# Self-attention with unscaled exponentials: sums by a matmul with ones, outputs divided, transposes one step sooner

## What is computed

```python
x = x + tanh(g_xattn) * xattn(layernorm(x), ctx, Wq, Wk, Wv, Wo)
x = x + tanh(g_ffn) * ffn(layernorm(x), ...)
# in ffn:
q, k = rope(q, k)
scores = einsum('bqhd,bkhd->bhqk', q, k) * 32 ** -0.5
attn = softmax(where(causal, scores, min))
ctx = einsum('bhqk,bkhd->bqhd', attn, v)      # 8 batches, 16 heads, 100 x 100
x = x + ctx @ wo
# then the router, two of eight experts for each token, and a shared expert
```

## Time and profile before

| | before |
|---|---|
| median of 3 runs | 976.92 us (974.06 to 979.06) |
| the profiled execution | 981.73 us |
| its span, first to last instruction | 979.9 us |
| mean granted clock of TensorE | 0.956 of full speed |
| PE busy | 901.8 us (92%) |
| DVE busy | 654.4 us (67%) |
| ACT busy | 565.6 us (58%) |
| POOL busy | 397.8 us (41%) |

### The profile page before, as it was taken

The page is one execution under the profiler, slowest core; times in us unless marked ns, Lnnn a source line. Parts: engine busy times, 40 slices in busy tenths (PEclk is TensorE's granted clock), DMA queues, the critical chain, the costliest instruction groups (busy, mean ns, idle before and its releaser), DMA issues.

```text
span 979.9 us, 16173 instructions
## 1 busy us (share of the span) xinstructions
PE 901.8 (92%) x5713; PEld 836.0 (85%) x5713; DVE 654.4 (67%) x1466; ACT 565.6 (58%) x1455; POOL 397.8 (41%) x373
## 2 busy tenths in 40 slices
PE   5999999999999999999879888799857989999996
PEld 4889999999989999999857766598857989999896
DVE  3557776742637777742696956666855788898863
ACT  3656666644546666653344756545335767777661
POOL 3432222345432322336654421044462555565431
PEclk9999999999999999999997989699978999999999
DMA  5766710025530000006322111022486989999875
GB/s 150 210 231 187 208 52 2 11 73 148 160 101 16 1 2 1 12 28 175 92 79 65 44 46 42 12 87 86 131 275 197 280 270 318 286 302 306 252 195 149
DMA packets 118040, 129.41 MB, mean 132 GB/s; under 512 B 13188, under 2 KB 81228, under 8 KB 117360
## 3 DMA queue, kind: packets, MB, share of 16 engines
q1 hardware_dynamic: 98862, 104.74, 34.6%
q0 software_dynamic: 5120, 10.22, 5.2%
q10 hardware_dynamic: 13978, 13.41, 4.7%
HBM read 110.81 MB, written 26.19 MB: 140 GB/s over the span
## 4 chain that ended last, share of the span: by engine, by line
PE 61%; DVE 16%; DMA 9%; issue 5%; ACT 5%; POOL 3%; ACTq 0%; POOLq 0%; DVEq 0%; SPq 0%
PE bank L2012 55%; PE bank L2141 4%; DMA s_sum<-yo,target 2%; DMA eraw<-in_L_ffn_w_down_e_dram 2%; DVE we L1339 2%; ACT we L905 1%; DVE PQ L1520 1%; POOL s_rows L1942 1%; DMA s_rows<-HR,idx 1%; DVE HR L1336 1%; DVE PQ L1518 1%; DVE sm L1543 1%; DMA eraw<-in_L_ffn_w_gate_e_dram 1%; DMA sums<-s_sum 1%; DVE wf L1339 1%
## 5 line engine op out<-in xcount | busy, mean ns | idle before, releaser
L1902 POOL TENSOR_SCALAR SC<-SC,mx,anyv 100x361 f32<-100x361 f32 x128 | 81.4, 646 | 211.2 <-DVE mx L1451 200.9
L1873 POOL TENSOR_TENSOR wf<-raw,wf 128x512 fp32r<-128x512 f32 x54 | 72.6, 1350 | 138.2 <-ACT wf L891 138.2
L1885 POOL TENSOR_TENSOR we<-eraw,we 128x704 fp32r<-128x704 f32 x40 | 74.1, 1852 | 99.5 <-ACT we L905 99.4
L1873 POOL TENSOR_TENSOR wx<-raw,wx 128x512 fp32r<-128x512 f32 x64 | 83.2, 1311 | 76.0 <-ACT wx L891 75.8
L905 ACT ACTIVATE we<-eraw 128x704 fp32r<-128x704 f32 (+2 forms) x140 | 96.8, 718 | 28.1 <-DMA eraw<-in_L_ffn_w_down_e_dram 13.1
L1339 DVE TENSOR_TENSOR we<-eraw,we 128x704 fp32r<-128x704 f32 (+2 forms) x100 | 92.8, 944 | 22.6 <-ACT we L905 22.4
L2012 PE MATMUL bank<-H2h,wf 128*128 128x400 f32 x352 | 99.7, 351 | 0.0
L1021 ACT ACTIVATE SC<-SC,mx 100x361 f32<-100x361 f32 x128 | 75.4, 593 | 29.3 <-DVE mx L1447 28.9
L2012 PE MATMUL bank<-XTh,wx 128*128 128x400 f32 x256 | 72.3, 356 | 3.7 <-POOL wx L1873 2.3
L1339 DVE TENSOR_TENSOR Kl<-bank,Kh 128x362 fp32r<-128x362 f32 x64 | 34.1, 535 | 60.3 <-ACT Kh L979 60.3
L1339 DVE TENSOR_TENSOR QOl<-bank,QOh 128x200 fp32r<-128x200 f32 (+1 forms) x96 | 41.5, 432 | 46.2 <-ACT QOh L934 36.2
(11 more groups left out here) (259 smaller groups left out, 2784.0 us busy)
## 6 DMA issues: line engine op xcount, KB each, us to landing
raw<-s_unit SPq DMA_DIRECT2D x60, 256.0 KB, 3.7
eraw<-in_L_ffn_w_gate_e_dram SPq DMA_DIRECT2D x40, 352.0 KB, 4.1
eraw<-in_L_ffn_w_up_e_dram SPq DMA_DIRECT2D x40, 352.0 KB, 5.4
eraw<-in_L_ffn_w_down_e_dram SPq DMA_DIRECT2D x40, 256.0 KB, 5.8
raw<-in_L_xattn_Wq_dram SPq DMA_DIRECT2D x32, 256.0 KB, 3.1
raw<-in_L_xattn_Wo_dram SPq DMA_DIRECT2D x32, 256.0 KB, 2.9
s_rows<-Z SPq DMA_DIRECT2D x6, 800.0 KB
XB<-s_rows ACTq DMA_DIRECT2D x18, 256.0 KB, 5.6
```

The costliest lines, as they stand in the source:

```text
L1873: eng.tensor_tensor(w[:, 1, :, :], raw[plan.raw[stream, u] % 4][:, :, :], f32(w[:, 0, :, :]), ALU.subtract).then_inc(sem("pool_w"), 1)
L1885: eng.tensor_tensor(w[0:rows, 1, 0:n], eraw[u % 6][0:rows, 0:n], f32(w[0:rows, 0, 0:n]), ALU.subtract).then_inc(sem("pool_e"), 1)
L1902: eng.tensor_scalar(sc, sc, m[:, 3, h:h + 1], anyv[:, b:b + 1], ALU.mult, ALU.mult).then_inc(sem("pool_p"), 1)
```

## The change

The exponentials are no longer scaled by the inverse of their sums before the transposes. ACT's exponentials drop the accumulated sums; DVE's reciprocal of 100x4 and its multiply of 100x400 go. Instead `f_out` is made in two parts of two columns of heads each, in steps `4q + 6` and `4q + 7`. In each part four matmuls with a tile of ones (`ones32`, 100x32) write the sums of the exponentials into one half of bank 4, spread over the 32 partitions of their head, and eight matmuls write the outputs into the other half. DVE takes the reciprocal of the 128x200 sums and multiplies the 128x200 outputs into an SBUF tile `CD` (two of them); ACT copies it to `CXh`, and DVE, one step later, subtracts for `CXl`, now from two SBUF tiles. The next part waits until the last one is divided out of bank 4.

The transposes move from step `u + 3` to `u + 2`, wait for the exponentials alone, and all use bank 3, so each waits for the copy of the one before. On ACT the exponentials now stand first in a step, then the copy of the turned rows, then `CXh`. No DMA moves. POOL fills `ones32` with one memset early on, and the counts that wait for its constants shift by one. Where the later stage takes over banks 3 and 4 it waits for `dve_ft` and `dve_cd`.

```diff
@@ steps and tables
-CONST = {"zero": 1, "eps": 3, "pad": 7, "causal": 10, "router": 11, "numbers": 19, "orders": 25, "split": 27}
+CONST = {"zero": 1, "eps": 3, "pad": 7, "causal": 10, "router": 11, "ones": 12, "numbers": 20, "orders": 26, "split": 28}
...
+    CDS = Region(nc, A2.at, A2.end)
+    CD = CDS.ring("CD", 2, [128, 2, T])
+    ones32 = CDS.place("ones32", [T, FD])
@@ -1091,28 +1094,26 @@
                            scale=scale).then_inc(sem("act_f"), 1)
 
         def self_attention(n):
-            u = n - 3
+            if n < 32:
+                act.wait_ge(sem("dve_fn"), n + 1)
+                if n >= 4:
+                    act.wait_ge(sem("pe_ft"), n - 3)
+                p, m, bank = PF[n % 4], sm[n % 4], score_bank[n % 4]
+                for c in range(4):
+                    e = eng.activation(p[:, c, :], bank[0:T, c * T:(c + 1) * T], ACT.Exp, bias=m[:, c:c + 1], scale=-1.0)
+                e.then_inc(sem("act_fe"), 1)
+            u = n - 2
             if 0 <= u < 32 and u % 2 == 0:
                 act.wait_ge(sem("pe_ft"), u + 1)
                 if u >= 6:
-                    act.wait_ge(sem("pe_fo"), (u - 6) // 4 + 1)
-                eng.activation(flat(PTf[u % 6][:, :, :]), banks[3 + u % 2][0:T, 0:4 * T], ACT.Copy).then_inc(sem("act_ft"), 1)
-            u = n - 4
-            if u >= 0 and u % 4 == 3:
-                h, b = divmod(u // 4, HB)
-                act.wait_ge(sem("pe_fo"), u // 4 + 1)
-                src = banks[4][:, 0:4 * T].rearrange("p (a b) -> p a b", a=4)
-                eng.activation(CXh[h][:, :, batch_slice(b)], src, ACT.Copy).then_inc(sem("act_cx"), 1)
-            u = n
-            if u < 32:
-                act.wait_ge(sem("dve_fn"), u + 1)
-                if u >= 4:
-                    act.wait_ge(sem("pe_ft"), u - 3)
-                p, m, bank = PF[u % 4], sm[u % 4], score_bank[u % 4]
-                for c in range(4):
-                    e = eng.activation(p[:, c, :], bank[0:T, c * T:(c + 1) * T], ACT.Exp, bias=m[:, 1, c:c + 1],
-                                       scale=-1.0, accum_out=m[:, 2, c:c + 1])
-                e.then_inc(sem("act_fe"), 1)
+                    act.wait_ge(sem("pe_fo"), 2 * ((u - 6) // 4 + 1))
+                eng.activation(flat(PTf[u % 6][:, :, :]), banks[3][0:T, 0:4 * T], ACT.Copy).then_inc(sem("act_ft"), 1)
+            if n >= 6 and n % 4 >= 2:
+                part = 2 * ((n - 6) // 4) + n % 2
+                h, b = divmod(part // 2, HB)
+                act.wait_ge(sem("dve_cd"), part + 1)
+                at = slice(part % 2 * 2, part % 2 * 2 + 2)
+                eng.activation(CXh[h][:, at, batch_slice(b)], CD[part % 2][:, :, :], ACT.Copy).then_inc(sem("act_cx"), 1)
 
         def po(h, m):
             act.wait_ge(sem("pe_po"), h * KD + m + 1)
@@ -1538,34 +1539,43 @@
             m, bank = sm[u % 4], score_bank[u % 4]
             dve.wait_ge(sem("pe_fs"), u + 1)
             if u >= 4:
-                dve.wait_ge(sem("dve_fp"), u - 3)
+                dve.wait_ge(sem("act_fe"), u - 3)
             src = bank[0:T, 0:4 * T].rearrange("p (a b) -> p a b", a=4)
-            eng.tensor_reduce(m[:, 1, :], src, AX, ALU.min).then_inc(sem("dve_fn"), 1)
+            eng.tensor_reduce(m[:, :], src, AX, ALU.min).then_inc(sem("dve_fn"), 1)
+
+        def low_of(part):
+
+            h, b = divmod(part // 2, HB)
+            at = slice(part % 2 * 2, part % 2 * 2 + 2)
+            dve.wait_ge(sem("act_cx"), part + 1)
+            low(CXl[h][:, at, batch_slice(b)], CD[part % 2][:, :, :], CXh[h][:, at, batch_slice(b)]).then_inc(sem("dve_cx"), 1)
 
         def self_attention(n):
             if n == 0:
                 f_max(0)
-            u = n - 3
+            if n >= 7 and n % 4 in (3, 0):
+                low_of(2 * ((n - 7) // 4) + (n + 1) % 2)
+            u = n - 2
             if 0 <= u < 32 and u % 2:
                 dve.wait_ge(sem("pe_ft"), u + 1)
                 if u >= 6:
-                    dve.wait_ge(sem("pe_fo"), (u - 6) // 4 + 1)
-                eng.tensor_copy(flat(PTf[u % 6][:, :, :]), banks[3 + u % 2][0:T, 0:4 * T]).then_inc(sem("dve_ft"), 1)
-            u = n - 4
-            if u >= 0 and u % 4 == 3:
-                h, b = divmod(u // 4, HB)
-                dve.wait_ge(sem("act_cx"), u // 4 + 1)
-                src = banks[4][:, 0:4 * T].rearrange("p (a b) -> p a b", a=4)
-                low(CXl[h][:, :, batch_slice(b)], src, CXh[h][:, :, batch_slice(b)]).then_inc(sem("dve_cx"), 1)
-            u = n - 1
-            if 0 <= u < 32:
-                p, m = PF[u % 4], sm[u % 4]
-                dve.wait_ge(sem("act_fe"), u + 1)
-                chained(eng.reciprocal(m[:, 3, :], m[:, 2, :]))
-                r4 = m[:, 3, :].rearrange("p (a o) -> p a o", o=1).broadcast_to([T, 4, T])
-                eng.tensor_tensor(p[:, :, :], p[:, :, :], r4, ALU.mult).then_inc(sem("dve_fp"), 1)
+                    dve.wait_ge(sem("pe_fo"), 2 * ((u - 6) // 4 + 1))
+                eng.tensor_copy(flat(PTf[u % 6][:, :, :]), banks[3][0:T, 0:4 * T]).then_inc(sem("dve_ft"), 1)
             if n + 1 < 32:
                 f_max(n + 1)
+            if n >= 6 and n % 4 >= 2:
+                part = 2 * ((n - 6) // 4) + n % 2
+                h, b = divmod(part // 2, HB)
+                dve.wait_ge(sem("pe_fo"), part + 1)
+                if part >= 2:
+                    dve.wait_ge(sem("dve_cx"), part - 1)
+                cd = CD[part % 2]
+                sums = banks[4][:, 2 * T:4 * T].rearrange("p (a b) -> p a b", a=2)
+                outs = banks[4][:, 0:2 * T].rearrange("p (a b) -> p a b", a=2)
+                chained(eng.reciprocal(cd[:, :, :], sums))
+                eng.tensor_tensor(cd[:, :, :], outs, cd[:, :, :], ALU.mult).then_inc(sem("dve_cd"), 1)
+            if n == 8 * HB + 3:
+                low_of(2 * B - 1)
 
         def er(h, i):
             b = h * HB + i
@@ -1907,6 +1917,7 @@
         def ffn_constants():
             pool.wait_ge(sem("pe_wo"), 32)
             eng.memset(WR[:, :, :], 0.0).then_inc(sem("pool_const"), 1)
+            eng.memset(ones32[:, :], 1.0).then_inc(sem("pool_const"), 1)
             for i in range(NE):
                 eng.memset(io8[:, :, i:i + 1], float(NE - i)).then_inc(sem("pool_const"), 1)
             eng.memset(ones[:, :], 1.0).then_inc(sem("pool_const"), 1)
@@ -2276,42 +2287,43 @@
                     if c == 3:
                         e.then_inc(sem("pe_fs"), 1)
 
-        def f_out(q):
+        def f_out(q, part):
 
             h, b = divmod(q, HB)
             pe.wait_ge(sem("act_ft"), 2 * q + 2)
             pe.wait_ge(sem("dve_ft"), 2 * q + 2)
             pe.wait_ge(sem("dve_v"), HB * (h + 1))
-            if q:
-                pe.wait_ge(sem("dve_cx"), q)
+            pe.wait_ge(sem("pool_const"), CONST["ones"])
+            if q or part:
+                pe.wait_ge(sem("dve_cd"), 2 * q + part)
             else:
                 pe.wait_ge(sem("dve_ht"), B - 1)
-            for c in range(4):
+            for i in range(4):
+                mm(banks[4][32 * i:32 * i + 32, 2 * T:4 * T], ones32[:, :],
+                   flat(PTf[(4 * q + i) % 6][:, 2 * part:2 * part + 2, :]), True, True)
+            for cc in range(2):
+                c = 2 * part + cc
                 for i in range(4):
                     at = (4 * c + i) * FD
-                    e = mm(banks[4][32 * i:32 * i + 32, c * T:(c + 1) * T], V[h][:, b, at:at + FD],
+                    e = mm(banks[4][32 * i:32 * i + 32, cc * T:(cc + 1) * T], V[h][:, b, at:at + FD],
                            PTf[(4 * q + i) % 6][:, c, :], True, True)
             e.then_inc(sem("pe_fo"), 1)
 
         def self_attention(n):
-            u = n - 3
+            u = n - 2
             if 0 <= u < 32:
-                pe.wait_ge(sem("dve_fp"), u + 1)
-                if u < 2:
+                pe.wait_ge(sem("act_fe"), u + 1)
+                if u == 0:
                     pe.wait_ge(sem("dve_v"), HB)
-                    pe.wait_ge(sem("dve_ht"), B - 1)
-                elif u % 2 == 0:
-                    pe.wait_ge(sem("act_ft"), u // 2)
+                elif u % 2:
+                    pe.wait_ge(sem("act_ft"), u // 2 + 1)
                 else:
                     pe.wait_ge(sem("dve_ft"), u // 2)
-                    if u >= 5:
-                        pe.wait_ge(sem("dve_cx"), (u - 5) // 4 + 1)
                 for c in range(4):
-                    e = eng.transpose(banks[3 + u % 2][0:T, c * T:(c + 1) * T], PF[u % 4][:, c, :], ident[0:T, 0:T])
+                    e = eng.transpose(banks[3][0:T, c * T:(c + 1) * T], PF[u % 4][:, c, :], ident[0:T, 0:T])
                 e.then_inc(sem("pe_ft"), 1)
-            u = n - 4
-            if u >= 0 and u % 4 == 3:
-                f_out(u // 4)
+            if n >= 6 and n % 4 >= 2:
+                f_out((n - 6) // 4, n % 2)
             if n == 0:
                 f_scores(0, 0)
             if n % 4 == 0 and n < 32:
@@ -2321,7 +2333,7 @@
 
```

(6 more changed lines are left out.)

## The result

| | before | after |
|---|---|---|
| median of 4 runs each | 977.99 us (974.06 to 979.9) | 999.95 us (997.12 to 1003.31) |
| ratio | | 1.0212, 95% interval 1.0183 to 1.0241 |
| profiled execution, span | 981.73, 979.9 us | 1000.78, 998.7 us |
| busy PE, DVE, ACT | 901.8, 654.4, 565.6 us | 910.7, 656.8, 554.4 us |
| mean granted clock | 0.956 | 0.954 |

What follows compares the result with a forecast made beforehand. DVE was taken to lead from 538 to 558 and 600 to 628 us, PE from 558 to 600. Terms 1.5 + 1.7 + 1.5 + 2.7 = +7.4 us on 976.9 gave 984.3 us, range 971 to 992 (8 in 10).

Steps and rivals of the forecast that it cites:

- four terms of the sum: Losses for 538 to 560, 560 to 600, 600 to 628 and 628 to 637 us: +1.5, +1.7, +1.5, +2.7 us.
- the middle readings: Estimates of one 128x200 reciprocal on DVE from smaller ones, 1.15 us and 1.4 us; 1.3 was taken between them.
- the cheap: Rival for all attention stages: reciprocal 0.36 us; 971.1 us if PE also keeps its clock, chance 0.14, otherwise 975.3, chance 0.15.
- dear rival: Rival for all attention stages: reciprocal at 8.5 ns an element, 0.55 us more each; 990.5 us, chance 0.20.
- Stage 538 to 560: Attention beside the second half's rotary work: division delays CXh, exponentials, copy and PE's transposes, twice; +1.5 us.
- The ring: In 538 to 560: division, CXh, weight and Q/K copies, exponentials, turned-row copy, transposes wait in a loop; PE idles 2.6 us.
- Stage 560 to 600: Stretch led by PE up to po: two further output parts, with steps 17 to 19 and po's wait even; +1.7 us.
- the first rival: All attention stages: division at 0.36 us and PE's upper clock held from 576 to 591; 971.1 us, chance 0.14.
- Stage 600 to 628: Stretch led by DVE: work +2.0 us, partly absorbed by 3 us of idle, rows' root waiting up to 1; +1.5 us.
- The end: 628 to 637 us, steps 33 to 35: second output part waits until the first is divided out of bank 4; +2.7 us.
- The second: All attention stages: reciprocal at 8.5 ns an element; +13.6, 990.5 us, up to 2 more if the clock falls; chance 0.20.
- The third: In 538 to 560 the ring doesn't close, giving up to 3 us back; sum +2.9, 979.8 us, chance 0.16.

Runs made afterwards that it cites:

- the filled version: Changed kernel with spare matmuls on PE, 56 each ahead of the transposes of steps 9 and 13 and 60 ahead of the first po group; 994.92 us, ratio 1.0157.

## Why the prediction was wrong

The direction and the places were right. All four terms of the sum were too small: the chain was priced as if PE ran at its upper clock inside it, and DVE's idle from 600 to 628 was taken to shrink where it grew.

- **Prices of the parts, right.** For the division 1.3 us was taken, 1.402 measured; the middle readings of the earlier trace rows were the right ones, and the prices of the cheap and the dear rival both fell. Measured growth from the four-element reciprocal (168 ns) is (1402 - 168) / 196 = 6.3 ns an element. An output part takes 0.82 us at the upper clock (538.24 to 539.06), 0.83 taken. The estimate of 1.67 us from the Trainium skill, VectorE: DVE Perf Modes, section "First, the fixed hardware budget", was too high. The prediction says that its rows do not reach that estimate, but the dearest of them, 8.5 ns an element, lay above it.
- **Stage 538 to 560, the step that failed: 1.5 forecast, 4.7 to 6.9 measured.** The ring was walked at the upper clock: 561.2 - 548.4 = 12.8 us a round, and with the clock held it does take 13.3. But PE's group, transposes and output part lie inside the ring, and behind an idle of 2.6 us they ran in part at the lower clock, which cost up to 2.7 us in the round from step 9 to step 13. The prediction had that only as "up to 2 more" in a rival and as zero in its sum, though it had seen the clock fall behind 1.56 us of idle. Second, "until there nothing it does is shorter" overlooked that it gets longer: with one bank for transposes PE waits 0.45 us in step 5 and 0.72 in step 6. 1.5 + 0.5 + 1.2 makes 3.2 of the 3.4 us that the filled version lost here (46.54 - 43.11).
- **Stage 560 to 600: 1.7 forecast, 3.1 to 3.25 measured.** The two output parts are there. The excess is again the clock behind the ring's idle: the second wait of 2.6 us stands right before this stretch, and the granted clock was 0.50 from 564.95 to 568.00. Filled, with the clock at 1.00, the stretch took 25.73: +1.7. From 578 to 592 the clock stood at 1.00, as the first rival wanted. That brought no gain on the sum, since po's wait became 3.44 us, not 2.7: the last division starts late, behind DVE's low part, copy and maximum.
- **Stage 600 to 628: 1.5 forecast, 4.5 measured.** DVE's work, +2.8 for +2.0, was nearly right. The sign of the idle was wrong: it was to absorb some of that work, and it grew by 3.1, for 2.6 us of it through ACT's queue behind CXh. The prediction names that wait for the rows' root, at "up to 1 us" (0.9 measured), but not the 1.7 us for H2h, and lets the idle that was there outweigh it.
- **The end: 2.7 forecast, 3.55 to 4.1 measured, 3.0 to 3.5 of it by the shared bank.** A wait of 1.93, then in the first trace a part at the lower clock (0.67 + 0.82 us from start to start).
- **How much of the divisions stands on the path.** The sum had eleven of sixteen; leaving them out gave back 87% of their time, as much as fourteen, the clock's part included.
- **Second and third rival.** The second's price of 8.5 ns an element did not come true. Its 990.5 us, or up to 2 more with the clock that it mentions last, came nearest, but by another way and still 7 us short. The third fell: the ring closed, twice.

## What to carry to other kernels

When an edit puts a serial step in front of an instruction in an engine's queue, price everything queued behind that instruction, and follow it until the loop closes; moving the waiting instruction one step back in program order was worth 7.5 us here with the division as slow as ever. An idle gap made on PE can be paid twice where PE's own work lies in the same loop, so price PE there at both clock levels. Filling a wait with spare matmuls paid here where PE was what ended last: in the stretch from po to the logits it bought 0.9 us while DVE led, and 5.6 after the division had left DVE.

## What the runs showed of the hardware

- DVE's reciprocal of 128x200 takes 1402 ns, a copy of the same shape 362. On ACT the logarithm and the exponential that replace it take 352 and 370 ns, one behind the other:

```profile
L1130 ACT ACTIVATE CD<-CD 128x200 f32<-128x200 f32 x14 | 5.2, 370 | 0.4
L1128 ACT ACTIVATE CD<-bank 128x200 f32<-128x200 f32 x14 | 4.9, 352 | 5.0 <-PE bank L2051 5.0
```

- The Trainium skill, ScalarE: Activation LUTs, section "What it computes", says to use VectorE's reciprocal in place of ScalarE's own function of that name. That function was not tried here; the pair above took half of VectorE's time, and no table load stands among these instructions and the row softmax's exponentials in the trace (the only one from 516 to 640 us is at 622.40, behind the last of them).
- The same idle of 2.6 us on PE was followed by mean granted clocks of 0.81, 0.88, 0.88 and 0.96 over the next round in four executions of the same instructions.
